# The first phase of a fused decoder layer reordered: idle products ahead of the first transposes, gate products in two lots, one visit of ScalarE to the exponentials

## What is computed

```python
x = x + attn(layernorm(x), ...)
# in attn, for all heads at once:
beta = sigmoid(x @ Wb.T).reshape(B, T, H) * 2.0
g = -exp(A_log) * softplus(x @ Wa.T + dt_bias)
# and for each head h of 8:
q, k, v = (silu(causal_conv4(x @ W.T)) for W in (Wq, Wk, Wv))
# then a recurrence over the tokens with exp(g), beta, q, k and v
```

## Time and profile before

| | |
|---|---|
| median of three runs | 607.36 us (607.34 to 610.03) |
| the profiled execution | 607.52 us, of which 605.7 us are its span |
| mean granted TensorE clock | 0.969 |
| TensorE busy | 555.8 us (92%) |
| VectorE busy | 453.8 us (75%) |
| ScalarE busy | 356.3 us (59%) |
| POOL busy | 39.5 us (7%) |
| first phase | until about 62.7 us |

### The profile page before, as it was taken

One profiled execution on the slowest core, in us unless ns is written; L12 is line 12 of the kernel. 1 busy time (PEld: TensorE's weight loads), 2 busy tenths in 40 slices (PEclk: granted clock), 3 DMA queues, 4 the chain that ended last, 5 costly groups with the idle time before them and its releaser, 6 DMA issues.

```text
span 605.7 us, 15275 instructions
## 1 busy us (share of the span) xinstructions
PE 555.8 (92%) x6440; PEld 374.1 (62%) x6440; DVE 453.8 (75%) x1064; ACT 356.3 (59%) x557; POOL 39.5 (7%) x69
## 2 busy tenths in 40 slices
PE   3879879999999999999999999999998989577997
PEld 1526337576757675766576667667665778465646
DVE  5658898797969787887788778878796525689563
ACT  1567575496559565946694668465864143287351
POOL 5341000100010001000100010010000000100000
PEclk9979999999999999999999999999997899968899
DMA  5001112101210211020002100210013300000002
GB/s 165 1 1 45 27 16 67 27 1 28 59 26 7 34 46 24 10 70 11 22 14 67 13 19 16 66 13 18 2 36 97 97 5 12 0 1 1 1 1 69
DMA packets 49700, 18.63 MB, mean 31 GB/s; under 512 B 39100, under 2 KB 48352, under 8 KB 49632
## 3 DMA queue, kind: packets, MB, share of 16 engines
q1 hardware_dynamic: 49632, 17.66, 12.1%
HBM read 14.49 MB, written 3.15 MB: 29 GB/s over the span
## 4 chain that ended last, share of the span: by engine, by line
PE 75%; DVE 13%; ACT 8%; issue 2%; DMA 1%; ACTq 0%; DVEq 0%
PE bank L1292 18%; PE bank L1342 7%; DVE acc L895 6%; PE bank L1468 5%; PE bank L1245 4%; PE bank L1472 4%; PE bank L1563 4%; PE bank L1345 3%; PE bank L1484 3%; PE bank L1361 3%; PE bank L1478 2%; PE bank L1480 2%; PE bank L1482 2%; PE bank L1427 2%; PE bank L1339 2%
## 5 line engine op out<-in xcount | busy, mean ns | idle before, releaser
L895 DVE SCALAR_TENSOR_TENSOR acc<-bank,cw,acc 128x508 f32<-128x508 f32 (+2 forms) x240 | 176.0, 738 | 37.1 <-ACT acc L597 32.8
L1292 PE MATMUL bank<-xnT,wq 128*128 128x512 f32 x320 | 156.5, 616 | 13.6 <-DVE acc L895 12.8
L1292 PEld LDWEIGHTS bank<-xnT,wq 128*128 128x128 f32 x320 | 57.2, 194 | 72.9 <-issue 45.0
L597 ACT ACTIVATE acc<-bank,cw 128x512 f32<-128x512 f32 x80 | 55.4, 692 | 55.4 <-PE bank L1292 55.3
L1342 PE MATMUL bank<-kq 128*128 128x384 f32 x128 | 50.2, 498 | 0.8 <-issue 0.8
L644 ACT ACTIVATE T<-bank 32x512 f32<-32x512 f32 (+1 forms) x32 | 18.9, 590 | 43.6 <-PE bank L1361 29.8
L612 ACT ACTIVATE vT<-acc 128x512 f32<-128x512 f32 x32 | 21.0, 669 | 37.5 <-DVE acc L895 37.4
L928 DVE SCALAR_TENSOR_TENSOR AM<-bank,rb,DT 128x384 f32<-128x384 f32 x64 | 37.7, 607 | 2.4 <-PE bank L1342 2.1
L1468 PE MATMUL bank<-xnT,wg 128*128 128x512 f32 x64 | 33.8, 655 | 0.0
L996 DVE SCALAR_TENSOR_TENSOR xres<-bank,f,xres 128x256 f32<-128x256 f32 x64 | 26.9, 477 | 8.6 <-PE bank L1472 8.3
L612 ACT ACTIVATE kq<-acc 128x512 f32<-128x512 f32 x48 | 31.3, 659 | 3.2 <-DVE acc L895 2.9
(11 more groups left out here) (245 smaller groups left out, 1076.7 us busy)
## 6 DMA issues: line engine op xcount, KB each, us to landing
wq<-in_w_qkv SPq DMA_DIRECT2D x8, 640.0 KB, 4.0
blocks<-AM SPq DMA_DIRECT2D x128, 8.0 KB, 1.5
xres<-in_x SPq DMA_DIRECT2D x2, 512.0 KB, 4.6
Yl<-in_y_init SPq DMA_DIRECT2D x8, 128.0 KB, 2.4
Bl<-blocks SPq DMA_DIRECT2D x8, 128.0 KB, 2.0
wg<-in_w_gate SPq DMA_DIRECT2D x8, 128.0 KB, 2.1
solved<-Yl SPq DMA_DIRECT2D x8, 128.0 KB, 2.1
Yc<-solved SPq DMA_DIRECT2D x64, 16.0 KB, 1.9
```

Of the source, the lines that this page charges most:

```text
L597: a(acc[:, u % RING, :, :], bank[6 + u % 2][:, :].rearrange("p (b l) -> p b l", b=4), ACT.Copy, scale=cw[:, t, 3:4]).then_inc(s_tap.next(f ...
L895: stt(w, ps[:, :, 0:L - s], cw[:, t, 3 - s:4 - s], w, ALU.mult, ALU.add).then_inc(s_cv.next(f"u{u}_{s}"), 1)
L1292: ins = mm(bank[6 + u % 2][:, :], wq[:, cc, t, :], xnT[:, cc, 512 * half:512 * half + 512], start=cc == 0, stop=cc == KC - 1)
```

## The change

In the order of the program:
- TensorE: after the wait for `w_ba` and ahead of `turn_half(0)` it waits for a new tile `idle` (zeroed by VectorE's first instruction) and multiplies it 50 times, 128x256 in bf16, into bank 7. Nobody reads the result.
- The gate products go in two lots: those of sequences 0 to 5 behind unit 1, those of 6 and 7 behind unit 2. `gates` is raised by the last.
- ScalarE: the SiLU of unit 0 goes ahead of tap 2. `decays`, `constants` and `steps_of_delta` become one block behind tap 2, with an activation Abs added in it. The copy of the steps goes behind tap 6 (`each_step`), TensorE's part of it behind unit 6.
- POOL loses the minimum, the difference and the addition of 2, and the sign is put on the 8 values of `al` ahead of the series. VectorE adds 2 and does its casts behind unit 2's convolution, where they stood behind unit 1's.
- TensorE's `dt0` and `dt1` go behind unit 7, `dt2` behind unit 8. ScalarE takes `dt0` and `dt1` ahead of tap 8, and `dt2` ahead of tap 9.

```diff
-FIRST_SCALAR_ORDER = ("+0 +1 +2 +3 -0 -1 -2 q0 +4 +5 -3 -4 +6 -5 q1 +7 dt0 +8 dt1 +9 dt2 cs nr -6 -7 -8 -9").split()
+FIRST_SCALAR_ORDER = ("+0 +1 -0 +2 +3 -1 +4 +5 -2 q0 -3 +6 -4 +7 -5 q1 dt0 dt1 +8 dt2 +9 cs nr -6 -7 -8 -9").split()
-FIRST_TENSOR_ORDER = ("0 1 2 3 4 5 6 dt0 7 8 dt1 9 dt2 ca cs nrm e1_0 ...
+FIRST_TENSOR_ORDER = ("0 1 2 3 4 5 6 7 dt0 dt1 8 dt2 9 ca cs nrm e1_0 ...
+        idle = sb("idle", [P, 2 * P], BF16)
# POOL
-            pk(gt(zz, raw[:, :, :], rep(dtb[:, :].rearrange("p (o h) -> p o h", o=1), 1, B), ALU.add))
-            gs(po, zz, 0.0, None, ALU.min)
-            pk(gs(raw[:, :, :], zz, 0.0, None, ALU.max))
-            gt(ez, raw[:, :, :], po, ALU.subtract).then_inc(s_preG.next("gz"), 1)
-            pool.wait_ge(s_preA.sem, s_preA.at("gexp"))
-            gs(ra, ez, 2.0, None, ALU.add).then_inc(s_preG.next("rs"), 1)
+            gt(zz, raw[:, :, :], rep(dtb[:, :].rearrange("p (o h) -> p o h", o=1), 1, B), ALU.add).then_inc(s_preG.next("gz"), 1)
+            pool.wait_ge(s_preG.sem, s_preG.at("gz"))
+            gs(raw[:, :, :], zz, 0.0, None, ALU.max)
+            pool.wait_ge(s_preA.sem, s_preA.at("aexp"))
+            gs(al[:, :], al[:, :], -1.0, None, ALU.mult)
...
-            pool.wait_ge(s_preA.sem, s_preA.at("aexp"))
-            pk(gt(po, po, rep(al[:, :].rearrange("p (o h) -> p o h", o=1), 1, B), ALU.mult))
-            gs(gl[:, :, :], po, -1.0, None, ALU.mult).then_inc(s_preG.next("gl"), 1)
+            gt(gl[:, :, :], po, rep(al[:, :].rearrange("p (o h) -> p o h", o=1), 1, B), ALU.mult).then_inc(s_preG.next("gl"), 1)
# ScalarE
                 act.wait_ge(s_preG.sem, s_preG.at("gz"))
+                a(sm[1][:, :, :], sm[0][:, :, :], ACT.Abs).then_inc(s_preA.next("abs"), 1)
+                act.wait_ge(s_preA.sem, s_preA.at("abs"))
                 a(sm[1][:, :, :], sm[1][:, :, :], ACT.Exp, scale=-1.0).then_inc(s_preA.next("gexp"), 1)
-
-            def constants():
-
...
-            def steps_of_delta():
-
...
-                            elif h == -1 and step == "+1":
+                            elif h == -1 and step == "+2":
                                 decays()
-                            elif h == -1 and step == "+2":
-                                constants()
-                            elif h == -1 and step == "+3":
-                                steps_of_delta()
-                            elif h == -1 and step == "+4":
+                            elif h == -1 and step == "+6":
                                 each_step()
# VectorE
+            v.memset(idle[:, :], 0.0).then_inc(s_busy.next("zero"), 1)
...
-                dve.wait_ge(s_preG.sem, s_preG.at("rs"))
+                dve.wait_ge(s_preA.sem, s_preA.at("gexp"))
+                lk(ts(sm[2][:, :, :], sm[1][:, :, :], 2.0, None, ALU.add))
                 v.reciprocal(sm[2][:, :, :], sm[2][:, :, :]).then_inc(s_preD.next("rr"), 1)
...
-                            if len(steps) == 3 * NU - 6 and h == -1:
+                            if len(steps) == 3 * NU - 9 and h == -1:
                                 gates()
# TensorE
-            def decays():
-
-                turned(1)
-                for b in range(B):
+            def decays(batches):
+
+                if batches[0] == 0:
+                    turned(1)
+                for b in batches:
                     for cc in range(KC):
                         ins = mm(bank[5][:, 24 * b:24 * b + 24], xnT[:, cc, L * b:L * b + L], wba[:, cc, :], start=cc == 0, stop=cc == KC - 1)
-                ins.then_inc(s_preP.next("gates"), 1)
-                pe.wait_ge(s_preG.sem, s_preG.at("zero"))
+                if batches[-1] == B - 1:
+                    ins.then_inc(s_preP.next("gates"), 1)
+                    pe.wait_ge(s_preG.sem, s_preG.at("zero"))
...
+            pe.wait_ge(s_busy.sem, s_busy.at("zero"))
+            for _ in range(50):
+                mm(bank[7][:, 0:2 * P], idle[:, 0:P], idle[:, :], start=True, stop=True)
             turn_half(0)
             turned(0)
...
-                            elif h == -1 and step == "1":
-                                decays()
-                            elif h == -1 and step == "4":
+                            elif h == -1 and step in "12":
+                                decays(range(*{"1": (0, 6), "2": (6, 8)}[step]))
+                            elif h == -1 and step == "6":
                                 steps_of_delta()
```

More of the change, by code:

```diff
@@ L89 @@
 E_STEPS = " ".join(f"e1_{2 * i} e1_{2 * i + 1} e2_{i}" for i in range(4))
-FIRST_SCALAR_ORDER = ("+0 +1 +2 +3 -0 -1 -2 q0 +4 +5 -3 -4 +6 -5 q1 +7 dt0 +8 dt1 +9 dt2 cs nr -6 -7 -8 -9").split()
+FIRST_SCALAR_ORDER = ("+0 +1 -0 +2 +3 -1 +4 +5 -2 q0 -3 +6 -4 +7 -5 q1 dt0 dt1 +8 dt2 +9 cs nr -6 -7 -8 -9").split()
 FIRST_VECTOR_ORDER = ("u u u u u u u u u u u u u u u u u u u u u u u u u u u u u u rb e1_0 e1_1 e2_0 e1_2 rq e1_3 e2_1 e1_4 "
                 "e1_5 e2_2 e1_6 e1_7 e2_3 vt0 vt1 vt2 vt3").split()
-FIRST_TENSOR_ORDER = ("0 1 2 3 4 5 6 dt0 7 8 dt1 9 dt2 ca cs nrm e1_0 e1_1 e2_0 e1_2 e1_3 e2_1 e1_4 e1_5 e2_2 e1_6 e1_7 "
+FIRST_TENSOR_ORDER = ("0 1 2 3 4 5 6 7 dt0 dt1 8 dt2 9 ca cs nrm e1_0 e1_1 e2_0 e1_2 e1_3 e2_1 e1_4 e1_5 e2_2 e1_6 e1_7 "
                 "e2_3 vt0 vt1 vt2 vt3").split()
@@ L334, in build @@
         s_preD = Signal(sem("vector_prologue"), PRE_D)
-        s_preA = Signal(sem("scalar_prologue"), ["sdev0", "sdev1", "x0", "x1", "raw", "gexp", "aexp", "eu", "sig", "steps"])
+        s_preA = Signal(sem("scalar_prologue"), ["sdev0", "sdev1", "x0", "x1", "raw", "abs", "gexp", "aexp", "eu", "sig", "steps"])
         s_preP = Signal(sem("tensor_prologue"), ["t0", "t1", "gates", "steps"])
-        s_preG = Signal(sem("pool_prologue"), ["zero", "twice", "bounds", "gz", "rs", "gl", "bparity"])
+        s_preG = Signal(sem("pool_prologue"), ["zero", "twice", "bounds", "gz", "gl", "bparity"])
         s_pch = sem("pool_chain")
+        s_busy = Signal(sem("idle_operand_ready"), ["zero"])
         UH = [(t, f) for f in range(2) for t in range(HT)]
```

## The result

| | before | after |
|---|---|---|
| median of the comparison's runs | 607.35 us (605.05 to 610.03) | 615.82 us (614.13 to 617.78) |
| profiled execution, its span | 607.52, 605.7 us | 617.78, 616.0 us |
| ratio after to before | | 1.0139 (1.0085 to 1.0193) |

The forecast was 611.3 with a range of 608.9 to 612.9. The sign is right and the size is not: the kernel lost more than twice what was predicted.

A forecast was written before the change was run, and what follows sets the result against it. TensorE (92% busy) was taken to set the kernel's pace, hand-overs between engines the first phase's. That phase's terms summed to +4.0 us, carried whole to the end: 611.3 us by the median, range 608.9 to 612.9.

The forecast's parts named there:

- The idle lot: First phase, TensorE: 50 products from 8.0 take 7.1 to 8.0 us; first transposes at 15.9, before at 9.00.
- to the gates: First phase, from the transposes to the last gate product: gates end at 27.6 us, before at 22.5.
- ScalarE's visit: First phase, ScalarE's block from reading the raw gates to the sigmoid: 4.5 us, tap 3 at 32.1, before 26.03.
- tap 5 to tap 8: First phase, ScalarE as the chain: 11.85 us, tap 8 at 50.7 (before 46.68), VectorE waiting 4 us for it.
- the lower end of its bound: Abs in ScalarE's block: a small activation (0.20 us) without a table load of its own; upper end 1.3 us more.
- POOL's lateness: First phase: POOL's rows come at 41.2, before 36.4; TensorE asks near 43.4, so 2.2 us of cover and no cost.
- To unit 5: First phase: unit 5 may start at 35.05 (before 30.11), TensorE idle 3.4 us, tap 5 at 38.85 (before 33.61).
- the fall taken in it: Granted clock falling to half in TensorE's 3.4 us gap, so unit 5 takes 3.75 us in place of 1.97.
- the rival: No fall of the clock in the gap ahead of unit 5: phase +2.2 us, total 609.6; chance 0.20.
- The range's low end: Total of 608.9 us: no clock fall ahead of unit 5 and 3.4 us until the lot's clock step up.
- The clock elsewhere: Rest of the kernel: clock falls lying otherwise against the work, worth 0.9 us either way; chance 0.04.

The follow-up runs named there:

- no_lot: The changed kernel without its 50 idle products, all else of the change kept: 607.13 us, 0.9976 of the kernel before.
- after_pad78: The changed kernel with 78 one-column products more, ahead of the wait for `w_ba` and of its own 50: 612.37 us, 1.0066 of the kernel before.
- before_pad128: The kernel before with 128 one-column products ahead of the wait for `w_ba`: 609.42 us, ratio 1.0015.
- after_128_first: The changed kernel with its lot replaced by 98 one-column and 30 256-column products ahead of the wait for `w_ba`: 607.17 us, 0.9976 of the kernel before.
- before_128_first: The kernel before with 98 one-column and 30 256-column idle products ahead of the wait for `w_ba`: 607.75 us, ratio 0.9974.
- after_again: The changed kernel itself, run once more in the rounds of the last three experiments: 614.3 us, 1.0111 of the kernel before.
- after_narrow: The changed kernel with its 50 idle products 128 columns wide in place of 256: 613.79 us, 1.0124 of the kernel before.
- lot_first: The changed kernel with its 50 idle products moved ahead of the wait for `w_ba`: 610.46 us, 1.0009 of the kernel before.
- before_pad50: The kernel before with 50 one-column products ahead of the wait for `w_ba`: 615.05 us, ratio 1.0098.
- before_pad100: The kernel before with 100 one-column products ahead of the wait for `w_ba`: 614.71 us, ratio 1.0118.
- before_lot: The kernel before with only the 50 idle products added, at the place the change gives them: 617.99 us, ratio 1.0139.
- before_pad25: The kernel before with 25 one-column products ahead of the wait for `w_ba`: 615.55 us, ratio 1.0103.

## Why the prediction was wrong

The shift of the first phase, whether the instructions are displaced by other than 0 or 256, the time from the last values of the first phase to head 5's milestone, and the measured difference (ratio less 1):

| kernel | shift, us | displaced | to head 5, us | measured |
|---|---|---|---|---|
| before | 0 | no | 345.3 | 0 |
| no_lot | +1.0 | no | 344.7 | -0.24% |
| after_pad78 | +3.2 | no | 345.5 | +0.66% |
| before_pad128 | +1.3 | no | 346.4 | +0.15% |
| after_128_first | -2.8 | no | 345.3 | -0.24% |
| before_128_first | -1.1 | no | 345.0 | -0.26% |
| after | +2.3 | yes | 348.8 | +1.39% |
| after_again | +2.6 | yes | 348.5 | +1.11% |
| after_narrow | +0.1 | yes | 347.4 | +1.24% |
| lot_first | -3.5 | yes | 347.3 | +0.09% |
| before_pad50 | -0.4 | yes | 347.7 | +0.98% |
| before_pad100 | +1.3 | yes | 349.4 | +1.18% |
| before_lot | +4.6 | yes | 349.3 | +1.39% |
| before_pad25 | -1.4 | yes | 356.0 | +1.03% |

(The 356.0 of `before_pad25` is of an execution of 617.07 us, above the median of that kernel: between 81 and 290 us its clock fell four times, for 3.4 us each, and its first six bursts stand still for 6.3 us. It is left out of the means below.)

The two groups do not touch: 344.7 to 346.4 us against 347.3 to 349.4, on the mean 345.3 and 348.3. The displacement costs 3.0 us over heads 0 to 5; the six bursts stand still for 3.3 (`lot_first`) to 4.8 us (after) together. A fit of the thirteen measured differences by shift and displacement (and a constant, -0.03%) gives 0.14% (0.8 us) for each us of shift and 0.99% (6.0 us, standard error 0.9) for the displacement; single kernels lie up to 0.4% off it. For the change that is 0.3 + 1.0 = 1.3%, and 1.39 and 1.11% were measured.

- *The idle lot, to the gates, ScalarE's visit, tap 5 to tap 8*: right. Lot 7.93 us, gate products done at 27.3 (27.6), tap 3 at 31.87 (32.1), a wait of 4.40 us for tap 8 (4). Abs took the lower end of its bound, and POOL's lateness cost nothing: its series ends at 39.1, `Gb` is there at 41.0, as said.
- *To unit 5*: the gap came (3.31 for 3.4), the fall taken in it did not. That term was +1.8 too much. It was not a matter of the gap's length: the same 3.31 us let the clock fall in `no_lot` and not in two executions of the kernel after. The chance of 0.20 for the rival was too low for what the rows could tell. (The range's low end was not rounded down as said: 611.3 less 1.8 and 0.8 is 608.7, not 608.9.)
- *The step that failed*: "No later stage is changed, so what the phase ends later or earlier by, the kernel does too." No line of a later stage is changed, but the place of every later instruction in TensorE's stream is. The lot's 50 products with their weight loads are 100 instructions, and they move the borders between packets. Before, those of heads 0 to 5 lay within the first ten products of the burst, where the packet had long been there, and 2 to 10 products past its end; after, they lie at product 80 to 88, where the packet comes too late. By the fit this is 6.0 us of the 8.5; by the milestones 3.0 of it are shown to arise in heads 0 to 5.
- *The clock elsewhere*, 0.9 us either way: too small. The last two heads took 119.0 us before, 125.1 after, 121.4 in the second profile of the same kernel; over the kernels 119.0 to 123.5 whole and 120.5 to 125.9 displaced, means 121.4 and 122.8. So 1.4 us of them may go with the displacement, less than the spread within either group, and two executions of the same kernel differ by 3.7 us here.

What stays open: 6.0 us by the fit against 3.0 and 1.4 in the profiled executions leaves 1.6 us whose place is not shown, not much beside the fit's error of 0.9. In displaced kernels TensorE waits for `Yd` in the last head (3.1 us after and in `before_pad50`, 2.7 in `after_again`; 1.4 in `no_lot` and `before_pad128`), and the granted clock behind it stays at half longer: in the stretch 12 to 18 us behind head 6's milestone it is 0.52 to 0.64 in six of the eight displaced kernels and 0.92 to 1.00 in five of the six others. But `after_narrow` and `before_pad25`, displaced, have 0.99 and 1.00, `after_128_first` has such a wait (3.7) and 0.67 without displacement, and I made no kernel that takes this wait away alone. That the breaks end with a packet's landing the DMA records show, and that their places follow the count of instructions the paddings show; why TensorE goes on only 1.4 us behind the landing, and what decides when a packet is started, no row shows. I did not try to move the border out of the bursts of one head only.

## What to carry to other kernels

An edit at the start of a program moves the instructions of all that follows; where a later stage has dense bursts of tiny products, compare their timelines for breaks ended by "issue" before the edit itself is judged, and try the same edit with padding that makes the displacement a full 256 instructions, which puts the borders back where they were. An experiment that does nothing but displace is the control that such a comparison needs: here 50 products of one column in an idle stretch cost 1%. Idle products that raise the clock have to end before the work they are for can start; even so they brought nothing here that the total shows, since `after_128_first` with them and `no_lot` without any both measure -0.24%.

## What the runs showed of the hardware

- A burst of products of 10 ns each breaks for 0.2 to 1.75 us where a packet border lies at product 13 to 121 of it, with a period of 256 TensorE instructions, and goes on 2.15 to 2.82 us behind the start of a packet (16,384 bytes, 0.88 to 1.48 us) and 1.19 to 1.60 us behind its landing (72 breaks in 14 traces). The 36 borders at product 2 to 10 whose packet was started 2.9 to 4.5 us before brought no break.
- In head 6 the pause is 0.97 to 1.75 us, the longest of the kernel but in `before_pad25`. SP's stores of the blocks keep the DMA engines busy at the same time, but the packet takes no longer for it, 0.88 to 1.38 us. It starts later: after, 0.23 us ahead of the burst, where it is 0.44 to 1.15 us in the heads before.
- A bf16 product of one column takes 28 to 30 ns (50 in 1.49 us, 128 in 3.57).
- The granted clock is no function of the gap: 3.31 us of rest let it fall in `no_lot` and `lot_first`, not in two executions of the kernel after, and in `after_pad78` (and once in `before_lot`) it fell while TensorE was busy without a break, both times close behind gate products. TensorE's timeline and a window of `after_pad78`:

```profile
23.72 2.92 PE L1293 MATMUL bank<-xnT,wq 128*128 128x512 f32 x4
28.01 5.36 PE L1293 MATMUL bank<-xnT,wq 128*128 128x512 f32 x8
```

```profile
26.00:28.00 2.00, 2.00 (x9) 1.55 (x8) 0.59 (x1) 0.69 (x1) 0.00 (x0) 0.50 0.00 0
```
